# Selective scan of a hybrid block: the drive of a sixth state per unit turned in from token-major form

## The reference

```
u, z = split(x @ W_in.T);  u = silu(conv4(u) + b)
dt, Bm, Cm = split(u @ W_x.T)            # 8, 16 and 16 columns
dt = softplus(dt @ W_dt.T + b_dt);  A = -exp(A_log)
h[t] = exp(dt[t] * A) * h[t-1] + dt[t] * Bm[t] * u[t]      # per d and n
y[t] = sum over n of h[t] * Cm[t]  + u[t] * D
out = (y * silu(z)) @ W_out.T
```

## Time and profile before

| | us |
|---|---|
| median of 3 runs | 2167.45 (2163.66 to 2169.38) |
| the profiled execution | 2173.64 |
| its span, first to last instruction | 2171.9 |
| scan stage, first to last scan instruction | 808.8 (from 791.0 to 1599.8) |
| TensorE matmul busy, whole span | 2030.4 (93%) |
| VectorE busy | 1497.3 (69%) |
| GpSimd busy | 1439.8 (66%) |
| ScalarE busy | 1192.4 (55%) |
| mean granted TensorE clock | 0.976 |

### The profile page before, as it was taken

How to read it: one execution, slowest core, us unless ns; L and a number is a source line. 1 busy time by engine, 2 the same in 40 slices (tenths; PEclk the granted TensorE clock), 3 DMA queues, 4 the chain that set the end, 5 groups by cost and what they waited for, 6 DMA issues and landing times. The chain is left out here.

```text
span 2171.9 us, 42651 instructions
## 1 busy us (share of the span) xinstructions
PE 2030.4 (93%) x14462; PEld 1550.9 (71%) x14463; DVE 1497.3 (69%) x2745; ACT 1192.4 (55%) x2383; POOL 1439.8 (66%) x972
## 2 busy tenths in 40 slices
PE   7998999999999989889998889898789999999998
PEld 5886547999999535556665556565554489999994
DVE  6887584333333579999999999999976833433335
ACT  5775323222222269999999888989833232222222
POOL 6774004777777239999999998989940057777660
PEclk9999999999999999999999999989899999999999
DMA  8000100000000422233222322322233000000004
GB/s 302 1 0 2 39 1 17 25 24 25 25 24 24 112 86 99 89 105 104 99 89 99 99 89 95 101 91 98 87 141 132 0 22 25 24 25 25 24 23 120
DMA packets 72343, 141.93 MB, mean 65 GB/s; under 512 B 9979, under 2 KB 43773, under 8 KB 70054
## 3 DMA queue, kind: packets, MB, share of 16 engines
q1 hardware_dynamic: 63142, 121.87, 16.8%
q0 software_dynamic: 9088, 18.63, 3.0%
HBM read 123.82 MB, written 16.65 MB: 65 GB/s over the span
## 5 line engine op out<-in xcount | busy, mean ns | idle before, releaser
L2206 POOL TENSOR_TENSOR m_seen<-m_state,experts 128x1024 f32<-128x1024 f32 x256 | 599.7, 2365 | 59.1 <-DVE m_state L2260 52.5
L2260 DVE TENSOR_TENSOR_SCAN m_state<-experts,ps 128x512 f32<-128x512 f32 x448 | 540.3, 1235 | 1.4 <-PE ps L1797 1.2
L1814 PE MATMUL ps<-ident,m_seen 128*128 128x128 f32 x2048 | 280.5, 282 | 36.8 <-POOL m_seen L2206 36.8
L1814 PEld LDWEIGHTS ps<-ident,m_seen 128*128 128x128 f32 x2048 | 244.3, 145 | 76.1 <-POOL m_seen L2206 56.0
L2019 ACT ACTIVATE experts<-delta,experts 128x512 f32<-128x512 f32 x448 | 291.4, 713 | 1.0 <-DVE delta L2286 0.5
L1528 POOL COPY f_weights<-experts 128x1898 f32 x142 | 252.3, 1777 | 23.9 <-issue 23.5
L1351 PE MATMUL first_up_ps<-f_xT,f_weights 128*128 128x128 f32 x1988 | 241.5, 275 | 1.5 <-issue 1.4
L1351 PE MATMUL ps<-zu,f_weights 128*128 128x128 f32 x1988 | 241.5, 275 | 1.5 <-issue 1.4
L1351 PEld LDWEIGHTS first_up_ps<-f_xT,f_weights 128*128 128x128 f32 x1988 | 233.2, 192 | 2.6 <-issue 2.6
L1351 PEld LDWEIGHTS ps<-zu,f_weights 128*128 128x128 f32 x1988 | 233.2, 192 | 2.6 <-issue 2.6
L2240 DVE TENSOR_TENSOR ps<-m_delta_u,ps 128x512 f32<-128x512 f32 x286 | 193.4, 676 | 13.0 <-PE ps L1772 12.5
(11 more groups left out here) (421 smaller groups left out, 3928.7 us busy)
## 6 DMA issues: line engine op xcount, KB each, us to landing
experts<-m_rows SPq DMA_DIRECT2D x144, 512.0 KB, 3.7
experts<-in_experts SPq DMA_DIRECT2D x17, 1461.0 KB, 18.7
tokens<-f_rows SPq DMA_DIRECT2D x8, 512.0 KB, 4.7
f_rows<-expert_out SPq DMA_DIRECT2D x8, 512.0 KB, 7.1
f_cols<-expert_out SPq DMA_DIRECT2D x8, 512.0 KB, 7.3
out<-X SPq DMA_DIRECT2D x4, 512.0 KB, 3.2
X<-in_x SPq DMA_DIRECT2D x4, 448.0 KB, 5.8
f_xin<-tokens,f_take POOLq DMA_INDIRECT x71, 2.6
```

The costliest lines, as they stand in the source:

```text
L1814: mm = pe.matmul(Y[:, i // 2, at:at + P], seen[:, n % SEEN, h, i * P:(i + 1) * P], ident[:], is_transpose=True, start=(n == 0 and at == 0) ...
L2206: pool.tensor_tensor(seen[:, n % SEEN], state[:, n % RING], c_rep[:, Q % C_RING, n % C_GROUP, :].unsqueeze(1).to_broadcast([P, HALF, SEG]) ...
L2260: dve.tensor_tensor_scan(state[:, n % RING, h, :], decay_, drive_, before_, ALU.mult, ALU.add).then_inc(s_state, 1)
```

## The change

State 13 is made an across state, so there are six in place of five, and eight ordinary ones. State 13's copies are issued at the end of step 9, where those of state 14 stood; state 14's are issued at the end of step 11.

```diff
@@ -1568,8 +1568,8 @@
                 RING, B_RING, SEEN, C_GROUP, C_RING, SCALED = 4, 2, 4, 2, 4, 2
                 AWAY = (4, 12)
                 AWAY_AT = {15: 4, 6: 12}
-                ACROSS = (2, 5, 8, 11, 14)
-                ACROSS_AT = {15: 2, 1: 5, 3: 8, 6: 11, 9: 14}
+                ACROSS = (2, 5, 8, 11, 13, 14)
+                ACROSS_AT = {15: 2, 1: 5, 3: 8, 6: 11, 9: 13, 11: 14}
                 TILES = SEG // P
                 DT_ROWS = RANK + 1
                 GROUPS = NS // C_GROUP
```

## The result

Before: 2169.28 us, median of 22 runs (2163.66 to 2174.98). Changed: 2173.59 us, median of 22 runs (2170.73 to 2178.47). The ratio is 1.002, with a 95% interval of 1.0013 to 1.0028: 4.3 us slower, under 0.3%, but not zero. The forecast was 0.6 us faster. The profiled execution of the changed kernel took 2170.89 us, with a span of 2169.1 us. That is 2.8 us less than the profiled execution of the kernel before, although its scan is 2.6 us longer: its scan begins at 786.6 us of the span, that of before at 791.0, and nothing ahead of the scan was changed. So the scan is compared here by its own units, and the whole kernel by the medians.

A forecast was written before the change was run, and what follows sets the result against it. The bound was taken as a loop through VectorE, GpSimd's products and TensorE's turns. Terms: -1.2 us (unit 15), +0.6 us (ScalarE), others 0; the resulting -0.6 on the median 2167.45 gave 2166.8 us, range 2160 to 2174.

The forecast's parts named there:

- The loop: Units 1 to 14: VectorE, GpSimd's products, TensorE's turns and next matmuls set the period; VectorE's saved drives gain 0.
- The wait of about 1 us before state 13's turns: TensorE at unit ends: its wait for GpSimd's product, 1.01 us in unit 11, would still be there.
- Unit 15: Last unit, with no next unit and no delta work on GpSimd: VectorE's two saved drives gain 1.2 us.
- ScalarE: Four added copies per unit, 1.6 us, absorbed by waits except in unit 1, which was charged 0.6 us.
- L1710 waits: TensorE's turn of the normalisation would wait about 2 us in units 0, 1 and 3.
- TensorE: Two matmuls fewer, eight transposes more per unit, some 0.4 us, hidden by two waits for GpSimd: cost 0.
- rival B: TensorE's clock falls in ten more unit ends, 1.6 us each: 16 us slower, 2183 us; chance 7%.
- two matmuls fewer: States 11 and 12 on TensorE: transposes replacing two 512-column matmuls might let the clock fall.
- a longer wait: States 14 and 15 on TensorE: the wait behind the added transposes grows, which might let the clock fall.
- dense transposes kept the full clock: Unit 5, 1075.7 to 1079.2: 33 matmuls, all but one transposes, at granted clock 0.99, argued against a fall.
- Rival A: VectorE is the bound in the scan, so its 18.6 us of saved drives are all gained: 2148.9 us; chance 6%.
- Rival C: ScalarE becomes the bound in units 0 to 6, its 1.6 us adding up to 11 us: 2178 us; chance 7%.

The follow-up runs named there:

- e10_warm_late: Changed kernel with redundant matmuls repeated in TensorE's idle time at unit ends, only from unit 7 on: 2164.58 us, ratio 0.9974.
- e11_warm_late_before: Kernel before the change with redundant matmuls repeated in TensorE's idle time at unit ends, only from unit 7 on: 2166.71 us, ratio 0.9984.
- e2_warm: Changed kernel with redundant matmuls repeated in TensorE's idle time at the ends of units throughout the scan: 2169.43 us, ratio 0.9993.
- e6_warm_before: Kernel before the change with redundant matmuls repeated in TensorE's idle time at the ends of units throughout the scan: 2163.93 us, ratio 0.9978.
- e4_turn_last: Changed kernel with TensorE's turns of GpSimd's products of states 12 to 15 moved behind the matmuls or turns for the next drive: 2148.5 us, ratio 0.9909.
- e5_turn_last_before: Kernel before the change with the same TensorE order as e4_turn_last: 2158.6 us, ratio 0.9948.
- e7_copies: Kernel before the change with only ScalarE's list altered: state 14's copies at step 9 and again at step 11: 2171.6 us, ratio 1.0010.
- The warmed kernels: Kernels with redundant matmuls filling TensorE's waits at unit ends; from unit 7 on, 2164.58 us with the change and 2166.71 us without.
- e13_changed_again: Changed kernel run once more, unaltered, for a second trace: 2173.48 us, ratio 1.0015 against the kernel before.
- e8_rows_back: Changed kernel with state 13's two bf16 matmuls issued again right ahead of its turns, which overwrite them: 2173.77 us, ratio 1.0017.
- e1_pace: Changed kernel with two useless 512-column products per unit on VectorE behind the scans of state 12: 2187.7 us, ratio 1.0085.
- e12_turn_last_ten: e4_turn_last with ScalarE's copies for state 14 at step 10 in place of 11: 2161.2 us, ratio 0.9958.

## Why the prediction was right in the mechanism and wrong in the sum

**The loop (right).** "What VectorE does in states 12 to 15 is beside this loop." VectorE's wait for L1772 went to 22.0 us, inside the 15 to 25 forecast, and VectorE's work in unit 11 fell by 1.0 us without a gain. With the low clock gone on both sides, units 8 to 14 are 351.7 us with the change and 351.6 without (e10_warm_late, e11_warm_late_before): the drives saved there are worth nothing in this order. The pair e2_warm and e6_warm_before says the same, 351.5 and 351.7. The wait of about 1 us before state 13's turns, forecast to stay, is 0.2 to 0.3 us at the ends of units 10, 12 and 14, where the slow turns of state 12 fill it. e4_turn_last and e5_turn_last_before show the other side: with the turns out of the loop, the same change gains 10 us.

**Unit 15 (right).** -1.2 us forecast, -1.3 measured.

**ScalarE (the sum right by luck).** +0.6 us forecast, +0.6 measured in units 0 to 7. But the forecast put it into unit 1, and unit 1 grew by 0.15 us (48.74 to 48.89), with ScalarE busy 0.9 us longer and not 1.6; 0.4 us are unit 0's, which differs by more between two traces of the same kernel. e7_copies has +1.8 us in the median (0 to 4.6). L1710 waits at most 1.3 us, not 2. And the forecast had overlooked one who waits. In units 0, 1, 3 and 5 the first scan of state 14 waits 1.5 us; unit 1 in time:

```profile
880.08 0.60 PE L1797 MATMUL ps<-ident,experts 128*128 128x128 f32 x4
881.81 0.20 ACT L2067 ACTIVATE experts<-m_state 128x4 f32<-128x4 f32 x1
882.10 1.22 DVE L2260 TENSOR_TENSOR_SCAN m_state<-experts,ps 128x512 f32<-128x512 f32 x1 [1.47 <-ACT experts L2067]
```

TensorE's turns for state 14 are over by 880.7, though they had waited 1.1 us for their copies. The scan goes when L2067 ends: this is `keep`, with which ScalarE saves the last column of states 10 and 11, whose slot of the ring of four the scan of state 14 overwrites. It stands behind the second gate half and the normalisation, so the added copies push it back. Little of this reaches the unit's length (+0.15 us in units 1 and 3, +0.3 in 5): the loop takes it in.

**TensorE (the step that failed).** "Behind them stand two waits for GpSimd of 1.22 and 1.01 us, which take them in: 0", and VectorE's longer wait "1.6 us, and the next unit starts when it did". Both look only at the order of ends. What was left out is what the same arrival does to TensorE in between: state 15's two matmuls, which had stood after a wait of 1.06 us and close before delta times u, run earlier, and their wait comes back as 1.01 us before L1789, next to the 1.22 us that was there. The granted clock then fell in seven unit ends for three. The warmed kernels price a fall, as their units 8 to 14 have none: before, (356.2 - 351.6) / 3 = 1.5 us each, about as rival B had it (1.6); changed, (359.4 - 351.7) / 7 = 1.1 us each. The difference is 7.7 - 4.6 = +3.1 us where the prediction had 0, and with +0.6 and -1.3 the scan comes out 2.4 us longer. The traces have 2.6; the medians have 4.3 in one comparison and 2.2 in the other (e13_changed_again), so the sum of the traces lies between the two.

That the clock costs these 3.1 us is shown, by e10_warm_late and e11_warm_late_before. What sets off the four more falls is shown only by exclusion: not the exchanged matmuls (e8_rows_back), not ScalarE's copies (e7_copies), which leaves VectorE's earlier arrival and the eight added transposes, which no run with that arrival leaves out. That it works through the pair of waits is argued, and unit 7, units 11 and 13, and e1_pace do not fit it. One rival is left untested. The low-clock stretches of unit ends keep a spacing of 51.2 us or whole multiples of it, in the changed kernel and in the one before (1239.6, 1290.8, 1444.4), so it may count where a unit's end lies in time as much as how long TensorE waits in it.

**Rival B** named this mechanism with 7%, at ten falls more and 16 us; four more came, about 3 us. Its reason, two matmuls fewer, was wrong, by e8_rows_back; its other one, a longer wait, fits six of the eight ends of units 7 to 14 and is not shown as the trigger. The argument against it, that dense transposes kept the full clock, still stands, but answered another question: at the unit ends TensorE was not dense, but waited. The rule of the Trainium skill on transposes (TensorE: Matmul & The Clock Gate, Part 4: PE-mode transpose), that they do not count as busy in the way matmuls do, gets no support from e8_rows_back. No run fills the waits with transposes in place of matmuls, which would test it there.

**Rival A** fell in this order: by the rule of the Trainium skill (Perfetto Trace Analysis, Identifying the Most-Contended Engine), the busiest engine was relieved, and the time went up. In the order of e4_turn_last the same relief gains 10 us. **Rival C** did not come, but unit 1 of e4_turn_last, at 48.89 us with 48.64 of ScalarE, shows it as the next bound of the early units.

What is still open: what sets off the fall of the clock; the cause of the 12.7 us in e12_turn_last_ten, which is read from its waits and was not tested by itself; and where the scatter of the kernel before (11 us) comes from. Part of it lies outside the scan: over the 14 traces the first scan starts anywhere from 784.8 to 791.0 us.

## What to carry to other kernels

When the busiest engine of a loop is relieved, follow the loop through all engines first: if it ends in waits for another engine, the saving turns into a longer wait, and only a change in what stands in front of the awaited instruction (here TensorE's turns behind the refills: 2158.6 for 2169.3 us by itself, 2148.5 with the change) makes it count. An engine that arrives earlier also moves the idle time of its neighbours; look at the granted clock wherever TensorE's waits have moved. Price an instruction that only moves by what its new neighbours then wait for.

## What the runs showed of the hardware

- A product on VectorE with both operands in SBUF, 128x512 f32, took 1.26 and 1.65 us beside GpSimd's products (e1_pace), against 0.68 us for the drive with one operand in PSUM. Even 224 columns took 1.13 us.
- Idle times of TensorE of 1.01 and 1.23 us around 1.09 us of transposes came with 3.4 us at 1.2 GHz, which began 0.3 us behind the second; with the first of them filled by matmuls, the same turns ran at full clock behind 1.22 us of idle time (e10_warm_late). In the changed kernel the low-clock ends of units 8 to 14 start at 1235.5, 1286.7, 1337.9 and so on to 1542.7, each 51.2 us after the last, though the units are 50.0 to 52.4 us long; units 11 and 12 together, and 13 and 14, take 102.4 us, twice that spacing. The second trace has the same, from 1236.6 us on. The same two waits at the end of unit 7 were followed by no low clock.
- Seven redundant matmuls per unit end (0.22 us each from start to start) gave back 4.6 us without the change and 7.7 us with it in units 8 to 14; the change itself moved these units by 3.2 us.
